# Choosing experts from unnormalised exponentials, and the order of work behind the last group

## The reference

```python
x = layernorm(x + attn(x))                 # RMS norm, gated recurrence, MLP
x = layernorm(x + xattn(ctx, ctx, x))      # causal convolution of outer products, 16 heads
x = layernorm(x + ffn(x))                  # the part that the change is about

# ffn: 64 experts, the 6 best of each token, at most 64 tokens per expert
logits = x @ gate_w.T
scores = softmax(logits)
topk_w, topk_idx = top_k(scores, 6)
# per expert: its first 64 tokens in order, d = (silu(buf @ w_gate) * (buf @ w_up)) @ w_down
y = einsum('tkh,tk->th', out_exp, topk_w)  # tokens beyond the 64 give 0
y = y + (silu(x @ sh_gate.T) * (x @ sh_up.T)) @ sh_down.T
```

## Time and profile before

| | us |
|---|---|
| three timed runs | 563.73, 564.67, 568.37 |
| median | 564.67 |
| the profiled execution, its own time | 562.52 |
| its span in the trace | 560.7 |
| TensorE matmuls busy | 516.0 (92%) |
| VectorE busy | 377.3 (67%) |
| ScalarE busy | 216.9 (39%) |
| Pool busy | 193.1 (34%) |
| mean granted TensorE clock | 0.986 of full speed |

### The profile page before, as it was taken

One profiled execution on the slowest core, in us unless ns is written; L12 is line 12 of the kernel. 1 busy time (PEld: TensorE's weight loads), 2 busy tenths in 40 slices (PEclk: granted clock), 3 DMA queues, 4 the chain that ended last, 5 costly groups with the idle time before them and its releaser, 6 DMA issues.

```text
span 560.7 us, 6906 instructions
## 1 busy us (share of the span) xinstructions
PE 516.0 (92%) x2211; PEld 317.7 (57%) x2211; DVE 377.3 (67%) x953; ACT 216.9 (39%) x440; POOL 193.1 (34%) x236
## 2 busy tenths in 40 slices
PE   7999999999999799999979999987879999998876
PEld 3438466754766554587744668754444555554565
DVE  2653246759775959786877975899855666663296
ACT  5484135722346841225844114610303333332043
POOL 4703400139024237021507303100026677744250
PEclk9999999999999989999989999998998999999999
DMA  7900993000001100010700010599997999996997
GB/s 269 338 3 23 414 402 136 1 25 13 2 0 39 56 15 23 1 39 0 249 1 1 0 37 2 193 316 294 272 264 231 322 337 331 317 314 221 374 417 260
DMA packets 39894, 91.83 MB, mean 164 GB/s; under 512 B 4513, under 2 KB 24385, under 8 KB 39729
## 3 DMA queue, kind: packets, MB, share of 16 engines
q1 hardware_dynamic: 34864, 75.45, 40.4%
q0 software_dynamic: 4992, 15.93, 8.8%
HBM read 67.02 MB, written 24.34 MB: 163 GB/s over the span
## 4 chain that ended last, share of the span: by engine, by line
PE 65%; DVE 22%; DMA 5%; issue 5%; ACT 2%; SPq 1%; POOL 0%; DVEq 0%; POOLq 0%
PE mb L781 17%; PE mb L1080 8%; PE kb L974 8%; DMA arena<-y_dram 4%; PE kb L1100 4%; PE kb L920 3%; PE kb L1098 3%; PE kb L809 2%; DVE arena L1160 2%; PE mb L787 2%; PE tb L787 2%; DVE arena L1146 2%; PE kb L800 2%; PE mb L800 2%; PE mb L832 2%
## 5 line engine op out<-in xcount | busy, mean ns | idle before, releaser
L781 PE MATMUL mb<-arena 128*128 128x512 f32 x320 | 140.2, 594 | 6.1 <-DVE arena L1201 5.4
L781 PEld LDWEIGHTS mb<-arena 128*128 128x128 f32 x320 | 60.3, 190 | 78.2 <-issue 69.6
L443 POOL TENSOR_TENSOR arena<-arena 128x256 f32<-128x256 f32 (+7 forms) x128 | 80.9, 665 | 66.2 <-PE mb L834 66.2
L673 ACT ACTIVATE arena<-mb,cols 128x512 f32<-128x512 f32 x24 | 16.5, 687 | 78.0 <-PE mb L781 77.9
L974 PE MATMUL kb<-arena 128*128 128x256 f32 x192 | 44.2, 381 | 1.9 <-DVE arena L1389 1.7
L974 PEld LDWEIGHTS kb<-arena 128*128 128x128 f32 x192 | 35.5, 190 | 9.5 <-DVE arena L1389 4.6
L1080 PE MATMUL mb<-arena,x3T 128*64 128x352 f32 x224 | 39.3, 472 | 0.0
L507 POOL DMA_INDIRECT y_dram<-shh,y_all x32 | 32.2, 1008 | 19.9 <-DVE shh L1539 12.2
L468 POOL TENSOR_TENSOR arena<-arena 128x1024 f32<-128x1024 f32 x4 | 9.4, 2350 | 84.6 <-DVE arena L1196 58.9
L1160 DVE TENSOR_TENSOR arena<-arena 128x1024 f32<-128x1024 f32 x28 | 35.9, 1284 | 0.5
L1389 DVE SCALAR_TENSOR_TENSOR arena<-mb,cols,arena 128x512 f32<-128x512 f32 x24 | 17.9, 744 | 24.0 <-PE mb L781 24.0
(11 more groups left out here) (243 smaller groups left out, 1016.3 us busy)
## 6 DMA issues: line engine op xcount, KB each, us to landing
arena<-in_w_experts_dram SPq DMA_DIRECT2D x28, 704.0 KB, 14.8
y_dram<-zeros SPq DMA_DIRECT2D x16, 768.0 KB, 11.0
arena<-y_dram SPq DMA_DIRECT2D x16, 768.0 KB, 16.7
arena<-in_w_experts_down_dram SPq DMA_DIRECT2D x56, 128.0 KB, 13.9
rows_dram<-rows POOLq DMA_DIRECT2D x4, 768.0 KB, 7.0
wextra<-in_w_experts_dram SPq DMA_DIRECT2D x4, 704.0 KB, 6.5
arena<-in_w_experts_down_dram SPq DMA_DIRECT2D x28, 96.0 KB, 14.6
arena<-in_x_dram SPq DMA_DIRECT2D x4, 512.0 KB, 3.6
```

Source lines behind the costliest of these rows:

```text
L443: last = e.tensor_tensor(v.kv[:, hb % 2, :, :, DOFF[d] * NB:DOFF[d] * NB + n], cx[:, :, :, 0:n], cx[:, :, :, d * NB:d * NB + n], ALU.mult)
L781: last = e.matmul(bank, w[:, c, n0:n0 + P], rhs[:, c, :], start=(c == 0), stop=(c == C - 1))
```

## The change

**The choice.** ScalarE's exp writes its result straight into `pp[:, :, 2:]`. `top_six` takes the eight largest from there, since a positive factor per token does not alter the order, and the exponentials are at most 1, below the 2.0 of the first columns. The sum and the reciprocal move behind the votes. One product remains, into `rows`, behind the mask. `rows_s` counts two per group, and `dve_r` six steps instead of seven; TensorE's waits for the votes go by the fourth.

**Behind the last group.** VectorE runs the eight rounds in one piece, then `firstd`, then two `shared_rows`, then the indices, then the third `shared_rows` and the sums. TensorE no longer runs half of `shared_down` and the zero matmuls ahead of the positions' transpose; all of `shared_down` stands behind it.

**The last block.** SP loads the rows of block 15 in two transfers, four rows of each token and then two, and TensorE waits for the second ahead of the fifth row.

```diff
 # sync_program
-        for b in range(NBLK):
+        for b in range(NBLK - 1):
             e.dma_start(v.yin[b], v.y_dram[b * P * TOPK:(b + 1) * P * TOPK, :].rearrange("(s k) d -> s (k d)", k=TOPK)).then_inc(s[f"load{b}"], 16)
+        b = NBLK - 1
+        for k, n, name in ((0, TOPK - 2, f"load{b}"), (TOPK - 2, 2, "last_y")):
+            e.dma_start(v.yin[b][:, k * D:(k + n) * D],
+                        v.y_dram[b * P * TOPK:(b + 1) * P * TOPK, :].rearrange("(s k) d -> s k d", k=TOPK)[:, k:k + n, :])\
+                .then_inc(s[name], 16)
...
-RDVE = 7
+RDVE, RVOTES = 6, 2
...
 # pool_program, rows_out
-            wait(e, s["rows_s"], g + 1)
+            wait(e, s["rows_s"], 2 * g + 2)
...
 # act_program
-                e.activation(v.logit[:], v.logit[:], ACT.Exp).then_inc(s["exp_s"], 1)
+                e.activation(v.pp[:, :, 2:], v.logit[:], ACT.Exp).then_inc(s["exp_s"], 1)
...
 # pe_program, in step (twice) and behind the groups (with G)
-                wait(e, s["dve_r"], RDVE * gt)
+                wait(e, s["dve_r"], RDVE * gt - RVOTES)
...
         shared_up(G - 1, 2, [(s["voteT_s"], G)] * 2)
-        e.wait_ge(s["shh_s"], NF * G)
-        shared_down(G - 1, [0])
-
-        keep_clock(mb[0], 4)
         e.wait_ge(s["pick_s"], PDVE * (G - 1) + 17)
         e.transpose(tb[0][:, 0:P], v.firstd[:].rearrange("p k n -> p (k n)"), v.ident[:]).then_inc(s["pickT_s"], 1)
-        shared_down(G - 1, [1])
+        e.wait_ge(s["shh_s"], NF * G)
+        shared_down(G - 1, [0, 1])
         e.wait_ge(s["idx_s"], 2)
         e.wait_ge(s["sh_s"], 2 * G)
-        e.wait_ge(s["shh_s"], NF * G)
...
             for k in range(TOPK):
+                if b == NBLK - 1 and k == TOPK - 2:
+                    e.wait_ge(s["last_y"], 16)
...
 # dve_program, top_six
-            n = r.did(e.tensor_reduce(v.sm, v.logit[:], AX.X, ALU.add))
-            wait(e, sem_r, n)
-            n = r.did(e.reciprocal(v.sm, v.sm))
-            wait(e, sem_r, n)
-            pv = v.pp[:, :, 2:]
-            n = r.did(e.tensor_tensor(pv, v.logit[:], v.sm[:, :, None].to_broadcast((P, NB, E)), ALU.mult))
-
-            wait_apart(e, v, sem_r, n)
             for b in range(NB):
                 last = e.max(v.m8[:, b, :], v.pp[:, b, :])
             n = r.did(last)
-            e.tensor_tensor(v.rows[:, :, D:D + E], v.logit[:], v.sm[:, :, None].to_broadcast((P, NB, E)), ALU.mult)
             wait_apart(e, v, sem_r, n)
...
+            pv = v.pp[:, :, 2:]
+            n = r.did(e.tensor_reduce(v.sm, pv, AX.X, ALU.add))
             wait(e, sem_r, n)
+            n = r.did(e.reciprocal(v.sm, v.sm))
             e.scalar_tensor_tensor(out=v.mask, in0=v.pr[:, :, 2:], scalar=0.0, in1=v.votes[:], op0=ALU.is_lt, op1=ALU.min)\
                 .then_inc(s["rows_s"], 1)
+            wait(e, sem_r, n)
+            e.tensor_tensor(v.rows[:, :, D:D + E], pv, v.sm[:, :, None].to_broadcast((P, NB, E)), ALU.mult)\
+                .then_inc(s["rows_s"], 1)
...
 # dve_program, behind the groups
-        rounds(0, 2)
-        for f in range(2):
-            shared_rows(G - 1, f)
-        rounds(2, 4)
-        shared_rows(G - 1, 2)
-        rounds(4, 8)
+        rounds(0, 8)
...
         psteps.did(last)
-        epilogue(nc, e, v, lambda: shared_sums(G - 1))
-def epilogue(nc, e, v, last_sums):
+        for f in range(2):
+            shared_rows(G - 1, f)
+        epilogue(nc, e, v, lambda: shared_rows(G - 1, 2), lambda: shared_sums(G - 1))
+def epilogue(nc, e, v, last_rows, last_sums):
...
     e.tensor_scalar(v.ybase[:], v.idx_all[:], float(TOPK), None, ALU.mult).then_inc(s["ybase_s"], 1)
+    last_rows()
     last_sums()
```

More of the change, by code:

```diff
@@ L246, in build @@
             dve_r rows_s rows_out vote_tr voteT_s pick_s pickT_s odd_s idx_s shu_done shg_s shh_s shd_done sh_s sums_out
-            prob_s rank_s yi_s u_in pool_f sum_pool g_tr gT_s gu_done sg_s he_s ht_done heT_s dn_done dout_s sum_pe sum_dve stats_s aggr_s fsd f_s out_s isA_s isB_s isF_s shF_s mx_s consts_s ybase_s""".split()
+            prob_s rank_s yi_s u_in pool_f sum_pool g_tr gT_s gu_done sg_s he_s ht_done heT_s dn_done dout_s sum_pe sum_dve last_y stats_s aggr_s fsd f_s out_s isA_s isB_s isF_s shF_s mx_s consts_s ybase_s""".split()
         for n, count in (("load", WRING), ("gat", RING), ("scat", DRING)):
@@ L1047, in _ @@
         e.wait_ge(s["sh_s"], 2 * (G - 1))
-        e.wait_ge(s["dve_r"], RDVE * G)
+        e.wait_ge(s["dve_r"], RDVE * G - RVOTES)
         votes_by_expert(G - 1)
```

## The result

| | before | changed |
|---|---|---|
| median of 20 runs each | 565.36 us | 561.61 us |
| lowest, highest | 562.5, 568.4 | 559.2, 564.8 |
| profiled execution, its span | 562.52, 560.7 | 561.55, 559.6 |
| PE, DVE, ACT, Pool busy | 516.0, 377.3, 216.9, 193.1 | 513.4, 374.3, 217.0, 194.3 |

The ratio of the times is 0.9924, with a 95% interval of 0.9906 to 0.9943: 0.8% faster, some 4.3 us (3.2 to 5.3); the two medians alone are 3.75 us apart. The forecast was 562.2 us, a change of -2.5 us or a ratio of 0.9956: the time is met within 0.6 us, the change was larger than forecast.

The account below looks back on a forecast made before the run. TensorE, busy for 92% of the span, was taken as the bound, with the chain through VectorE's choice and a relay behind the last group. -0.9 - 1.6 + 0 = -2.5 us gave 560.0 profiled, 562.2 us as median; range 559.8 to 565.8.

Parts of the forecast that it names:

- Part 1: Choice of the six experts, groups 2 and 3: one instruction less on the chain, -0.9 us (-0.6 to -1.2).
- The lower bound that I named: Choice: only 0.3 us per group, if the next product waits for ScalarE's Exp of the first half.
- my upper bound: Choice: 0.6 us per group, if all five small waits shrink.
- Part 2: Behind the last group: indices 3.4 us earlier, less 1.7 for half clock, third `gate_up` at 424.8 for 426.4: -1.6 us.
- 1.7 us for the half clock: New `shared_down`: cost of half clock (1.2 GHz) expected after TensorE's idleness.
- My upper bound of 1.96: `shared_down`: cost of a half-clock stretch lying wholly under work, from 16 instructions taking 5.41 us against 3.45.
- The rival with the clock down throughout: `shared_down`: all 24 instructions at half clock, 5.2 us more, third `gate_up` at 428.3; 565.7 us, chance 0.14.
- an early fall and a cost of 0.9 us: `shared_down`: if the lone transpose counts for nothing, clock falls early in the 6 us; sum 0.8 us larger.
- Gathers bind: Behind the last group: clock does not fall or recovers in idleness, `place_rows(0)` near 419.6; 561.3 us, chance 0.14.
- Gathers land late: Behind the last group: landing 7.5 us after issue, further gaps before the third `gate_up`; 563.8 us, chance 0.08.
- Part 1 does not arrive: Choice: next product waits for ScalarE or Pool as before, both groups keep their times; 563.1 us, chance 0.10.
- The split: Last block's two transfers: forecast 0; if the block did bind, at most 1.7 us hidden.

Follow-up runs that it names:

- the gaps filled: Changed kernel plus three zero matmuls behind `shared_up` and three behind the positions' transpose; 563.03 us, ratio 0.9965 to before.
- part 1 alone: Kernel before with only the choice changed (exp into `pp`, sum and product behind the votes); 564.98 us, ratio 0.9991.
- without the split: Changed kernel without the last block's two transfers; 560.10 us, ratio 0.9899 to before.
- both edits together: Changed kernel plus zero matmuls in the two gaps behind the last group and three weight loads held until the second gather landed; 578.44 us, ratio 0.9918.
- held loads: Changed kernel with weights of three pairs requested only when the second gather has landed; 578.41 us, ratio 0.9878 to before on that chip.
- the hold: Changed kernel plus zero matmuls in the two gaps and three pairs' loads held until the eighth gather landed; 570.65 us, ratio 1.0082 to before.
- part 3 alone: Kernel before with only the last block's rows loaded in two transfers; 565.74 us, ratio 1.0006.

## Why the prediction was right, and where it was not

The time (562.2 for 561.61), the verdict of less than 1% and the mechanism of each part held. The change did not: -2.5 us is a ratio of 0.9956, outside the measured 0.9906 to 0.9943. That the time is met within 0.6 us is in part luck: it was counted from a median of 564.67 over three runs, which over twenty is 565.36, and the sizes of two terms were off in opposite directions.

- **Part 1, the product into `pp` gone.** Forecast -0.9, 0.45 in each of two steps, bound 0.6. Measured 0.59 and 0.61: -1.2. The lower bound that I named, ScalarE's exponentials, did not bind (0.21 us of wait at L1329, without effect). The product's end follows Pool's sum by 0.56 us, as I had argued, and Pool's sum moved with the choice; of the 0.59 us, 0.44 are the instruction and the rest are smaller waits, my upper bound. What the sum left out is the clock ahead of `w_out`. The product ran at half clock in 7 of 16 cases instead of 5 of 6; at 1.69 us each that would be (1.67 - 0.88) x 1.69 = 1.3 us in the mean. But with so few executions, and with the other ordering by the time of the start, that is an estimate and not shown. I had both durations in the earlier trace rows, and used them only for `shared_down`.
- **Part 2, the early end of the search.** Forecast: the votes' transpose 0.44 earlier, `idx_all` 3.4 earlier, TensorE idle twice for almost 3 us, full clock in `gate_up`. Measured 0.35, 3.4, 3.08 and 2.56, and 1.40 us in each `gate_up`. `shared_down` starts at +19.7, as forecast (412.95 less 393.28).
- **The term that was mis-sized: 1.7 us for the half clock.** I took the loss from the 16 instructions of the earlier trace rows, one stretch of some 3.4 us. (My upper bound of 1.96 set a row of the timeline against one of the chain; timeline against timeline it is 5.41 - 3.72 = 1.69.) The rows of the changed kernel show 6.8 us at 0.50. The loss is 8.34 - 5.46 = 2.9 us against the same 24 at full clock with the gaps filled. My bounds were 0.9 and 1.96, so it lies outside. The rival with the clock down throughout (5.2 us lost) goes further wrong on the other side. `place_rows(0)` came at +28.9 for +27.3, the third `gate_up` at +33.4 for +31.5. Of these 1.9 us the clock is 1.2; the 24 instructions at full clock are 0.26 (5.46 for 5.2), and the steps from `place_rows(0)` to the third `gate_up` are 0.3 (4.5 for 4.2). Against the profile of before, part 2 won nothing: +0.3 where -1.6 was forecast.
- **What the clock did in the gaps.** It was granted in full for 5.0 us after TensorE ran dry at 405.5, and was at half from 410.6 on. The Trainium skill ("TensorE: Matmul & The Clock Gate", the part on the clock gate) has half rate as the default that only sustained activity lifts, and from it I had worked out an early fall and a cost of 0.9 us. The trace does not bear that price out: the fall came near the end of the idleness, and 5.9 of its 6.8 us lay under work. That the lone transpose did not keep the clock up agrees with that page of the Trainium skill.
- **Why the total still came out**, as far as the traces go. The profiled execution of before stood at the lower end of the twenty, 562.52 for a median of 565.36. Its gathers landed 3.9 us behind their issue. In the two other executions with the old order it took 6.0 and 6.4 us, and the third `gate_up` started at +36.0 and +36.1 instead of +33.1. With the new order and no further edit of this stage it was +33.4, +33.6, +33.8 and +32.9. So the early issue seems to give the gathers room: their landing no longer binds, or binds at the same height as the sums. The gain of part 2 would then be in the mean over executions and not in the profiled one. Three profiles of the old order against four of the new make this likely, and do not show it. Carrying the 2.2 us from profile to median over to the changed kernel covered it by accident: the changed kernel's profile and median are the same to 0.1 us.
- **The rivals.** *Gathers bind* is true under one condition: it holds as soon as the clock does not fall, as the filled gaps show. *Gathers land late* had the landing right and its effect wrong: 8.1 us behind the issue, past both the rival's 7.5 and my 3.0 to 7.2, and the sums at half clock still ended later. *Part 1 does not arrive* seems true for part 1 alone (0.9991), since late gathers and the half clock behind them take the gain back; it does arrive with part 2 in place. *The split* was worth nothing that shows, alone and in company. (The lower end of my range, 559.8, does not come out of its parts either: 561.0 less 0.9 is 560.1.)

**The sum of the parts.** Alone they give -0.5, -2.4 and +0.3, each uncertain by some 1.6 us: -2.6, uncertain by some 2.7. Together they gave -4.3 (3.2 to 5.3), and on another chip -6.0 (3.8 to 8.1) and, without the split, -5.7 (3.5 to 7.9). The surplus is thus not clear of the noise, or barely so, and it compares chips. For it I have an argument: part 1's time in front of the last group only counts when part 2 has taken the gathers off the path. With the numbers above, -1.2 (choice) - 1.3 (clock ahead of `w_out`) - 1.5 (third `gate_up` at a mean of +35.1 over three executions of the old order, against the changed kernel's +33.6 over two) is -4.0. The means rest on few executions each, so this is an account that fits, and not shown.

**Open.** Whether late gathers are why part 1 alone gave nothing in the median, and how much of the 4.3 us each part has. Why TensorE's signal came 3.2 us behind the recorded product with both edits together. And one chip, on which before took 583.5 us against 565.2 to 565.4 elsewhere: its loop took 147 us or more from the third `gate_up` on, even without held loads, with TensorE's waits mostly ahead of `down` and not of `gate_up`. Neither before nor the changed kernel was profiled on it, and the landings of weights in its traces are incomplete.

## What to carry to other kernels

Before a gap in TensorE's work is opened, price the half clock behind it for a stretch as long as the longest seen, and look for every other gap near the same length that the edit shortens. Where software-issued gathers share queues with bulk loads, the first took 3.1 us to land with the bulk held back and 5.9 to 8.5 us in seven of eight profiles with it in the queues (3.7 in the eighth, that of before), and when the queues came free differed between profiles; compare a profiled execution's time with the spread of the runs before resting a stage's sum on it. Before bulk loads are held back for gathers, count how much time the last of them has to spare: here it was 2.7 us, and the hold cost 14. And where a wait names no transfer, set the landings beside the starts of the work that waits.

## What the runs showed of the hardware that I had not expected

- Two idle stretches of 3.08 and 2.56 us with a 0.33 us transpose between gave 6.8 us at half clock, about double what one idle stretch of 3.54 us had given. Single idle stretches of 5.43 us (part 1 alone) and 5.00 us (part 3 alone) gave 6.8 us too.
- An idle stretch of 3.54 us was followed by half clock in 5 of 6 cases, one of 2.9 to 3.0 us in 7 of 16: the same code falls on either side from one execution to the next.
- The first gather took 7.6 to 8.5 us to land with a DMA share of 1.05 or 1.06 until it landed (changed kernel, its two profiles; gaps filled; without the split), and 3.1 us with the loads held back.
- VectorE's product of 512 elements beside Pool's sum took 1.93 to 2.27 us, against 0.69 alone, and ended 0.56 us behind the sum in both kernels and both groups.
- The same kernel took 565.2 to 565.4 us in three sets of runs, on two chips at least, and 583.5 on another.
